# Recurrent row scans and a normed, expanded convolution block: the reciprocal deviations by way of DRAM, square and norm on GpSimd, eleven VectorE taps, halves of channels first

## The reference, cut to what matters

```
pooled = x.mean((2, 3))                        # (8, 64)
hdn    = LN(pooled @ w_fc1.T)                  # 16 wide
dyn_w  = hdn @ w_fc2.T                         # a 5 x 5 filter for each image and channel
out    = depthwise_conv(x, dyn_w)              # 5 x 5, pad 2
out    = (out - mean_c) * rsqrt(var_c + eps)   # over the 64 channels of a pixel
out    = ln2_w * out + ln2_b
out    = gelu(w_expand @ out)                  # 64 -> 256 channels
gx     = sqrt(sum over h, w of out^2)          # per image and channel
nx     = gx / (mean over channels of gx + eps)
out    = gamma * (out * nx) + beta + out
result = w_shrink @ out + x                    # 256 -> 64 channels
```

## Time and profile before

| | |
|---|---|
| median of 3 runs | 893.47 us (891.79 to 895.72) |
| the profiled execution | 893.85 us |
| its span, first to last instruction | 892.0 us |
| mean granted TensorE clock | 0.971 |
| PE busy | 816.9 us, 92%, 5639 instructions |
| PEld busy | 666.5 us, 75% |
| DVE busy | 604.4 us, 68%, 1127 instructions |
| POOL busy | 454.5 us, 51%, 443 instructions |
| ACT busy | 433.2 us, 49%, 520 instructions |
| block two begins | about 505 us |

### The profile page before, as it was taken

How to read it: one execution, slowest core, us unless ns; L and a number is a source line. 1 busy time by engine, 2 the same in 40 slices (tenths; PEclk the granted TensorE clock), 3 DMA queues, 4 the chain that set the end, 5 groups by cost and what they waited for, 6 DMA issues and landing times. The chain is left out here.

```text
span 892.0 us, 16129 instructions
## 1 busy us (share of the span) xinstructions
PE 816.9 (92%) x5639; PEld 666.5 (75%) x5639; DVE 604.4 (68%) x1127; ACT 433.2 (49%) x520; POOL 454.5 (51%) x443
## 2 busy tenths in 40 slices
PE   5999999999999999999999675889999999999775
PEld 5999999999999999999999654455454555545231
DVE  4666666666666666678888657777887778888722
ACT  5690005777750000000000154798989898988662
POOL 2333333333323333368888466767777776765500
PEclk9999999999999999999999788889999999999997
DMA  6750000000000000000000100110222222223123
GB/s 139 170 141 0 0 0 1 0 0 0 0 1 1 0 0 0 1 1 0 0 0 0 47 0 24 34 36 24 48 47 47 47 47 47 47 47 71 24 48 71
DMA packets 51189, 26.99 MB, mean 30 GB/s; under 512 B 40720, under 2 KB 49104, under 8 KB 51152
## 3 DMA queue, kind: packets, MB, share of 16 engines
q1 hardware_dynamic: 51152, 26.51, 13.2%
HBM read 9.98 MB, written 8.39 MB: 21 GB/s over the span
## 5 line engine op out<-in xcount | busy, mean ns | idle before, releaser
L487 PE MATMUL psum<-line_hi,taps_hi 128*128 128x256 f32 x1270 | 203.0, 292 | 11.8 <-DVE taps_lo L383 8.6
L501 PE MATMUL psum<-line_lo,taps_hi 128*128 128x256 f32 x1270 | 202.5, 291 | 0.8 <-DVE line_lo L436 0.8
L495 PE MATMUL psum<-line_hi,taps_lo 128*128 128x256 f32 x1270 | 202.0, 291 | 0.0
L436 DVE SCALAR_TENSOR_TENSOR line_lo<-psum,rest 128x256 fp32r<-128x256 f32 x254 | 108.2, 426 | 123.6 <-POOL rest L263 115.3
L487 PEld LDWEIGHTS psum<-line_hi,taps_hi 128*128 128x128 f32 x1270 | 177.1, 192 | 13.0 <-issue 9.3
L501 PEld LDWEIGHTS psum<-line_lo,taps_hi 128*128 128x128 f32 x1270 | 176.4, 191 | 2.0 <-DVE line_lo L436 1.8
L495 PEld LDWEIGHTS psum<-line_hi,taps_lo 128*128 128x128 f32 x1270 | 176.7, 191 | 0.0
L263 POOL TENSOR_TENSOR rest<-x,line_hi 128x256 f32<-128x256 f32 x127 | 82.9, 653 | 168.5 <-DVE line_hi L427 168.5
L709 POOL TENSOR_TENSOR part<-part,prod 128x960 f32<-128x960 f32 (+2 forms) x64 | 145.2, 2269 | 24.3 <-ACT part L764 17.5
L315 ACT ACTIVATE by_h<-x (+1 forms) x128 | 85.7, 670 | 106.1 <-DVE x L416 104.5
L263 POOL TENSOR_TENSOR rest<-by_h,line_hi 128x256 f32<-128x256 f32 x127 | 91.5, 721 | 83.4 <-DVE line_hi L427 83.4
(11 more groups left out here) (129 smaller groups left out, 899.3 us busy)
## 6 DMA issues: line engine op xcount, KB each, us to landing
stage<-in_x_dram SPq DMA_DIRECT2D x32, 256.0 KB, 4.1
out_dram<-x SPq DMA_DIRECT2D x32, 256.0 KB, 4.4
crossed<-x SPq DMA_DIRECT2D x16, 256.0 KB, 3.5
crossed<-x SPq DMA_DIRECT2D x16, 240.0 KB, 3.6
fc_in<-in_L_conv_w_fc_dram SPq DMA_DIRECT2D x2, 100.0 KB
taps<-in_L_conv_k_td_dram SPq DMA_DIRECT2D x2, 80.0 KB, 3.3
taps<-in_L_conv_k_dt_dram SPq DMA_DIRECT2D x2, 80.0 KB, 3.3
taps<-in_L_conv_k_lr_dram SPq DMA_DIRECT2D x2, 80.0 KB, 3.5
```

Of the source, the lines that this page charges most:

```text
L436: dve.scalar_tensor_tensor(out=line_lo[:, (slot + 1) % SLOTS, :, part], in0=as_lines(line_ps[slot][:, 0:LINE]), scalar=0.0, in1=as_lines(r ...
L487: mm = pe.matmul(line_ps[slot][:, 0:LINE], taps_hi[:, s, d, :], line_hi[:, slot, :, d:d + WP], start=(d == 0), stop=(d == OFFSETS - 1))
L495: pe.matmul(line_ps[slot][:, 0:LINE], taps_lo[:, s, d, :], line_hi[:, slot, :, d:d + WP], start=False, stop=False, skip_group_check=True)
L501: mm = pe.matmul(line_ps[slot][:, 0:LINE], taps_hi[:, s, d, :], line_lo[:, slot, :, d:d + WP], start=False, stop=(d == OFFSETS - 1), skip_ ...
```

## The change

- `DVE_TAPS` has eleven taps, `ACT_TAPS` four: ("up", 3) goes from ScalarE and GpSimd to VectorE.
- `square` goes from ScalarE to GpSimd, behind `add_inner`. `norm` goes from VectorE to GpSimd, one instruction for the unit instead of two; it stands behind the first addition of products.
- `widen` and its constant `spread` are gone. SP writes `rstd` to a scratch in DRAM, waits until it is there, and loads it back over the channels into `rstd_wide` (`spread_rstd`), for unit s - 1 in slot s. SP then stores, and then loads `crossed`.
- `expand` and `gelu` go over the halves m of the channels outside and c inside. From the second expand of unit 14 on three pairs of banks take turns. `add_squares(e, 0)` follows the second gelu, `add_squares(e, 1)` opens the next slot. It writes to `dump`, a buffer of its own.
- `inner` has two buffers instead of three; `normed` has two whole units.
- `respond` writes to a free column of `stat_ps`; it stands one slot later by unit (n = s - 3 in place of e), the same slots as before. On TensorE it follows conv(3), on VectorE it stands ahead of four taps instead of one.

```diff
-            ("down", 3), ("cross", 2)]
+            ("down", 3), ("up", 3), ("cross", 2)]
-SIDES = [("up", 1), ("down", 1), ("up", 3)]
+SIDES = [("up", 1), ("down", 1)]
...
-        INNERS = 3
+        INNERS = 2
+        EXP_SETS = 3
+        FREE_CONV = 4 * (UNITS - 2)
...
+        def exp_set(e):
+            first = 4 if e < FREE_CONV else (4, 0, 2)[(e - FREE_CONV) % EXP_SETS]
+            return psum[:, first:first + 2, :]
...
+            def spread_rstd(u):
+                sp.wait_ge(rstd_ready, u + 1)
+                if u > 1:
+                    sp.wait_ge(rstd_spread, 32 * (u - 1))
+                sp.dma_start(rstd_dram[u % 2], rstd[:, u % 2, :]).then_inc(rstd_stored[u % 2], 16)
+                sp.wait_ge(rstd_stored[u % 2], 16 * (u // 2 + 1))
+                if u > 0:
+                    sp.wait_ge(normed_ready, u)
+                rows = rstd_dram[u % 2].rearrange("(g q) n -> g (q n)", g=4)
+                for h in range(2):
+                    mine = rows[:, SUBS * h * STAT_COLS:SUBS * (h + 1) * STAT_COLS].rearrange("(a g) n -> a g n", a=1)
+                    sp.dma_start(rstd_wide[C * h:C * h + C, :].rearrange("p (g n) -> p g n", g=4),
+                                 mine.to_broadcast([C, 4, SUBS * STAT_COLS])).then_inc(rstd_spread, 16)
...
             for s in SLOTS_RUN:
+                if s - 1 in range(UNITS):
+                    spread_rstd(s - 1)
+                if s >= 5:
+                    store(s - 5)
                 if s + 2 < UNITS:
                     cross(s + 2)
-                if s >= 5:
-                    store(s - 5)
...
+            def square(u):                                  # POOL
+                pool.wait_ge(inner_ready, u + 1)
+                if u > 0:
+                    pool.wait_ge(stats_done, u)
+                image = inner[:, u % INNERS, :, :].rearrange("p j w -> p (j w)")
+                pool.tensor_tensor(squares[:, :], image, image, ALU.mult).then_inc(squared, 1)
+            def norm(u):                                    # POOL
+                pool.wait_ge(rstd_spread, 32 * (u + 1))
+                if u > 1:
+                    pool.wait_ge(exp_done, 4 * (u - 1))
+                image = inner[:, u % INNERS, :, :].rearrange("p j w -> p (j w)")
+                pool.tensor_tensor(normed[:, u % 2, :], image, rstd_wide[:, :], ALU.mult).then_inc(normed_ready, 1)
...
-            for u in range(UNITS):
+            for s in range(UNITS + 2):                      # POOL
+                w, e = s - 1, s - 2
+                if w in range(UNITS):
+                    add_inner(w)
+                    square(w)
                 for n in range(1, N_ACT):
-                    add_product(u, n)
-                if u + 2 < UNITS:
-                    split_low(u + 2)
-                if u % 2 == 0 and u // 2 + 1 < B:
-                    make_dyn(u // 2 + 1)
-                add_inner(u)
+                    if s < UNITS:
+                        add_product(s, n)
+                    if n == 1 and e >= 0:
+                        norm(e)
+                if s + 2 < UNITS:
+                    split_low(s + 2)
+                if s % 2 == 0 and s // 2 + 1 < B:
+                    make_dyn(s // 2 + 1)
...
+                if n in range(UNITS):                       # ACT, n = s - 3
+                    add_squares(n, 1)
                 if 2 <= s + 2 < UNITS:
                     split_high(s + 2)
...
+                if s + 1 < UNITS:
+                    product(s + 1, 0)
                 if w in range(UNITS):
                     square_mean(w)
                     root(w)
+                if n in range(UNITS) and n % 2 == 1:
+                    root_energy(n // 2)
+                for i, between in enumerate(((1, 2), (), (3,), ())):
+                    if e in range(UNITS):
+                        gelu(e, i // 2, i % 2)
+                    if i == 1 and e in range(UNITS):
+                        add_squares(e, 0)
+                    for p in between:
+                        if s + 1 < UNITS:
+                            product(s + 1, p)
...
+                take(2)                                     # DVE, n = s - 3
                 if v >= 0:
                     finish(v, 0)
                 take(2)
+                if n in range(UNITS) and n % 2 == 1:
+                    sum_energy(n // 2)
                 if w in range(UNITS):
                     make_var(w)
                 take(1)
                 if w in range(UNITS):
                     make_rstd(w)
                 take(1)
+                if v >= 0:
+                    finish(v, 1)
+                take(1)
+                if n in range(UNITS) and n % 2 == 1:
+                    respond(n // 2)
                 take(N_DVE)
...
+                at_v(0)                                     # PE: shrink(v, 0)
                 conv(0)
                 conv(1)
+                if w in range(UNITS):
+                    statistics(w)
+                at_e(0, 0)                                  # expand(e, m, c)
+                at_v(1)
                 conv(2)
+                at_e(0, 1)
                 conv(3)
+                if n in range(UNITS) and n % 2 == 1:
+                    respond(n // 2)
+                at_e(1, 0)
                 conv(4)
                 conv(5)
+                at_e(1, 1)
```

More of the change, by code:

```diff
@@ L582, in block_two @@
         rstd = sb("rstd", [P, 2, STAT_COLS])
-        normed = sb("normed", [P, 2, COLS])
+        rstd_wide = sb("rstd_wide", [P, UCOLS])
+        normed = sb("normed", [P, 2, UCOLS])
+        dump = sb("dump", [P, 2 * UCOLS], BF16)
         wide = sb("wide", [P, HALVES, 2, WIDE, UCOLS])
@@ L629, in block_two @@
         rstd_ready = sem("rstd_ready")
-        wide_done = sem("wide_done")
+        rstd_stored = [sem(f"rstd_stored{i}") for i in range(2)]
+        rstd_spread = sem("rstd_spread")
         normed_ready = sem("normed_ready")
@@ L764, in product @@
                 act.activation(dst, src, ACT.Copy, scale=weight).then_inc(prod_ready, 1)
[L766 to L773, removed]
             def square_mean(u):
@@ L823, in _ @@
             for s in SLOTS_RUN:
[L824 to L829, removed]
+                w, e, n = s - 1, s - 2, s - 3
+                if n in range(UNITS):
+                    add_squares(n, 1)
                 if 2 <= s + 2 < UNITS:
                     split_high(s + 2)
[L833 to L839, removed]
+                if s + 1 < UNITS:
+                    product(s + 1, 0)
                 if w in range(UNITS):
@@ L898, in make_rstd @@
                 if u > 1:
-                    dve.wait_ge(wide_done, 2 * (u - 1))
+                    dve.wait_ge(rstd_stored[u % 2], 16 * (u // 2))
                 dve.reciprocal(rstd[:, u % 2, :], std[:, :]).then_inc(rstd_ready, 1)
[L902 to L909, removed]
             def sum_energy(b):
@@ L989, in take @@
                     taken[0] += n
-                if e in range(UNITS):
-                    norm(e, 0)
-                take(1)
+                take(2)
                 if v >= 0:
@@ L996, in _ @@
                 take(2)
-                if e in range(UNITS):
-                    norm(e, 1)
-                take(2)
-                if v >= 0:
-                    finish(v, 1)
-                if 0 < e <= UNITS and e % 2 == 0:
-                    sum_energy(e // 2 - 1)
-                take(2)
+                if n in range(UNITS) and n % 2 == 1:
+                    sum_energy(n // 2)
                 if w in range(UNITS):
@@ L1010, in _ @@
                 take(1)
-                if 0 < e <= UNITS and e % 2 == 0:
-                    respond(e // 2 - 1)
+                if v >= 0:
[3 more added lines that the diff above has]
+                    respond(n // 2)
                 take(N_DVE)
@@ L1075, in statistics, with expand @@
                             mm = pe.matmul(stat_ps[32 * g:32 * g + 32, n * STAT_COLS:(n + 1) * STAT_COLS],
[L1076 removed]
+                                           kept["pick"][:, SUBS - 1 - k:SUBS - 1 - k + 32],
                                            image[:, at:at + STAT_COLS], start=(k == 0), stop=(k == SUBS - 1))
                 mm.then_inc(stats_done, 1)
[L1080 to L1094 removed]
+            def expand(u, m, c):
+                e = 4 * u + 2 * m + c
+                if e == 0:
+                    pe.wait_ge(weights_ready, 1)
+                if c == 0 and m == 0:
+                    pe.wait_ge(normed_ready, u + 1)
+                if e == FREE_CONV + 1:
+                    pe.wait_ge(tap_step, N_DVE * UNITS)
+                if 0 < e <= FREE_CONV:
                     pe.wait_ge(gelu_done, e)
[L1096 to L1097 removed]
+                elif e >= FREE_CONV + EXP_SETS:
+                    pe.wait_ge(gelu_done, e - EXP_SETS + 1)
                 for hp in range(2):
                     half = slice(C * hp, C * hp + C)
[L1100 removed]
```

(34 more changed lines are left out.)

59 lines of the change are left out of this document (15 added, 44 removed).

## The result

The changed kernel takes 910.79 us (median of 4, 910.46 to 911.09), before it 893.37: ratio 1.0192, 95% interval 1.0177 to 1.0208. It is slower by 17.4 us, as forecast (903, range 885 to 913), by nearly twice the size forecast. Its profiled execution took 910.46 us, with a span of 908.7 and a mean granted clock of 0.944 (before 0.971).

What follows compares the result with a forecast made beforehand. No engine is full, so the order of waits binds. I(4) 612.4 plus 238.7 for slots 5 to 15, then 33.0 and 17.5, gave a span of 901.6 and the forecast 903 us, range 885 to 913.

Steps and rivals of the forecast that it cites:

- a longer ring: In each slot: GpSimd's additions and square, norm ending at 8.6, expand(0,0), shrink(v,1), finish, then VectorE's last taps.
- Odd slots: Mid-stage slots without respond: 18.8 us by the order of waits, 20.4 with 1.6 for the clock.
- The clock: TensorE idles ahead of expand(0,0) and its clock falls to 0.50: 1.6 us per odd slot, 1.0 per even.
- Even slots: Mid-stage slots that carry respond: 22.25 us by the order of waits, 23.25 with 1.0 for the clock.
- Respond's chain: VectorE's small respond instructions in even slots, ahead of the last taps: taken at 1.05 us.
- The scratch: SP's DRAM store (3.2) and loads: image there near 16.2, hidden by more than 8 us before that unit's norm.
- the tail: After I(15), the start of slot 15's completing addition of `inner`: 33.0 us to respond's matmul, then 17.5 to the end.
- Slots 0 to 4: I(0) 539.1, slots 1 and 2 about 16.2 each, 3 18.7, 4 22.3: I(4), slot 4's start, 612.4.
- The first: Rival: GpSimd multiplications cost what the addition costs, 0.37 x 2 per slot from 4 to 15: +9, 912 us; chance 0.18.
- The second: Rival: TensorE's clock holds in the idle stretch ahead of expand(0,0), 17.1 us fall out: 886 us; chance 0.24.
- third: Rival: VectorE's two stops are absent as TensorE comes earlier; VectorE's own work binds: 860 us; chance 0.06.
- the stops of 3.96 and 2.22: VectorE's waits forecast before finish(v,1), about 2 us plus the clock, and before respond in even slots, 2.4.

Runs made afterwards that it cites:

- experiment 1: shrink(v,1) put ahead of expand(0,0) on TensorE, against the changed kernel; 881.4 us, ratio to before 0.986.
- experiment 3: respond put ahead of the last tap on VectorE, TensorE's order unchanged, against the changed kernel; 890.1 us, ratio 0.997.
- experiment 2: The filler: eight extra f32 matmuls in TensorE's idle stretch ahead of expand(0,0), units 1 to 14, added to the changed kernel; 898.4 us, ratio 1.007.
- experiment 4: norm(s-2) put ahead of add_inner(s-1) on GpSimd, against the changed kernel; 890.7 us, ratio 0.998.
- experiment 10: The kernel of experiment 8 with the buffer `rstd_wide` beginning 8 bytes later; 852.0 us, ratio 0.954.
- experiment 5: The changed kernel with the moves of experiment 1 and experiment 3 together; 861.4 us, ratio 0.965.
- experiment 8: The changed kernel with the moves of experiment 1 and experiment 3, make_dyn in odd slots, and norm directly behind the square on GpSimd; 853.9 us, ratio 0.956.

## Why the prediction was right, and where its sizes were off

- **What bounds it.** Right: the wait of VectorE for `mean_sq` shrank from 3.79 to 0.43, ACT and PE have less work, and none of it became time, since the norm on GpSimd opens a longer ring. Experiments 1 and 3 show it by moving what waits behind the norm, without taking work away.
- **Odd slots**, forecast 20.4: 20.6 to 21.7, mean 20.9 over six. `norm` took 2.35 and not 2.01 (+0.34; the row nearest in shape was not nearest in price, had 2.38 for the addition too), `square` 1.89 (-0.12). The clock, 1.6 taken, cost 1.6 in slot 9 (expand 2.08 for 1.13, shrink 2.62 for 1.94 by its PE timeline); the prediction's 1.56 was read from a shrink that ran wholly at the lower level, where here it is expand and a part of shrink, so that the sizes agree so well is in part luck. In experiment 3 it cost 1.66 and 2.72.
- **Even slots**, forecast 23.25: 23.9. Four of five took 24.0. The term that was sized too low is the clock: 1.0 taken, 1.5 measured in slot 10 (expand 2.08 for 1.13, shrink 2.51 for 1.94). With 0.26 for the norm that makes 24.0. Respond's chain was 1.05 there, as forecast. In the fifth, slot 12, the clock held:

```profile
770.31:793.76 23.45, 20.63 (x113) 9.80 (x111) 18.44 (x23) 19.80 (x21) 17.70 (x9) 1.00 0.29 70
```

That is not the 22.5 which the forecast without the clock's term and with the norm's 0.26 would give, because the chain then meets GpSimd's diagonals (the TENSOR_SCALAR takes 1.19 instead of 0.17). So the prediction's 1.05 for the chain came true where the lower clock made respond late enough to miss the diagonals, which is luck; in slots 4 and 12, and with the filler, it failed. The prediction bounded GpSimd's instructions by themselves and not by what they do to VectorE's. The Trainium skill says it (SBUF — State Buffer, Terms, shared port pair): VectorE and GpSimd take turns on a pair of ports that is held for a full instruction, and the other blocks. Experiment 1's rows agree: 0.99 and 1.19 us for two elements, ending with GpSimd's.
- **The clock**, right in place and kind: PE idle 3.4 us ahead of the norm's end, at 0.50 by 715 (the earlier trace rows had the precedent). Experiment 2 shows that it is on the path: 12.4 us gained by adding work.
- **The scratch**, right that it is hidden. The single terms were off against each other: store 1.5 for 3.2 taken, loads 5.3 for 3.6 taken; the image was there at 16.4 in the tail (16.2 forecast). Its slack is smaller than "more than 8 us" suggests once the norm moves forward, as experiment 4 found out.
- **Slots 0 to 4 and the tail.** I(4) 612.4 forecast, 614.2 measured: slot 2 took 17.8 instead of 16.2, as GpSimd itself went into `add_inner` without idleness, slot 3 18.0 instead of 18.7, slot 4 23.5 instead of 22.3, where respond's chain was held by 1.2 (0.41 and 1.19 for 0.22 and 0.17). From I(15) to the end 50.5 forecast, 49.7 measured.
- **Rivals.** The first (multiplications at the addition's price) was half true: the norm is, the square is not. The second and third are excluded by the clock of 0.92 in the pair's window and by the stops of 3.96 and 2.22.
- **The sum** was 7.8 us low: 1.8 up to I(4), 6.1 in slots 5 to 15 (244.8 against 238.7; 2.9 of them because the norm ends at 8.86 and not 8.6, the rest mostly the clock), 0.6 around the span, and 0.8 the other way in the tail.

What stays open: why the clock held in some odd slots of experiment 3 and in slot 12 of the changed kernel and not in others, and what sets the price of GpSimd's multiplication (experiment 10). No run puts the same moves into the kernel before, with its five products on ScalarE. So experiments 5 and 8 show that the change's division of work can be 31 and 39 us faster than the kernel before as it stands, and not that this division is the better one.

## What to carry to other kernels

Here moving work off the busy engines paid nothing while the moved step stood late in the order of its new engine and others queued behind it: look first at what each engine issues right behind the step that waits. The same instructions in another order gave 57 us (910.8 to 853.9), three times what the change had cost. The stretch of idleness on TensorE cost twice, once as waiting and once as half clock on the work behind it, which VectorE waited for; work that is ready anyway belongs there (shrink in experiment 1).

## What the runs showed of the hardware that I had not expected

- A VectorE instruction of two elements that reads two SBUF operands, or a TENSOR_SCALAR on SBUF, lasts until a running GpSimd instruction ends: 0.99 and 1.19 us instead of 0.22 and 0.17 (experiment 1). Those with an operand from PSUM (the taps, 1.11 to 1.28 us beside GpSimd's work) and the RECIPROCAL of one element, 0.16 us beside GpSimd's diagonals, were not held.
- GpSimd's multiplication of 1024 f32 elements: 1.89 us with one operand twice, 2.35 to 2.38 with two different ones, 2.00 when `rstd_wide` begins 8 bytes and the buffers behind it 32 bytes later.
- TensorE at 1.2 instead of 2.4 GHz for part of a slot cost it 1.66 us (mean granted clock 0.92) and 2.72 us (0.84) in experiment 3, where the lower clock fell on expand and shrink, with the other engines unchanged. In experiment 2 a mean of 0.82 cost 0.24, since it fell on work that was not waited for.
- The DMA that reads 1 KB rows of a 64 KB scratch for 64 partitions each (256 KB) lands in 5.3 us, where the plain loads of 256 KB take 3.5; the store of 64 KB to DRAM lands in 1.5.
